# Moving the reloads of spilled FFN blocks from SyncE's queue to ScalarE's

## The chip, the cores and the metric

The kernel runs on one NeuronCore of a Trainium2 chip. Its time is device microseconds (us) from launch to end of one execution. A profile of one execution gives what each engine and each DMA queue did.

## The reference

The input x is 4 batches of 1024 tokens with 512 features. Each token gets a conditioned linear layer, then a two-layer network with simulated 8-bit quantization, then a residual sum:

```
relation = relu([x, mean(x), cond] @ W + b)               # 512 features
xq = round(relation / s_in) clipped to 0..255             # s_in = max(relation)/255
h  = relu(xq @ round(w1/s_w1).T  (scaled) + b1)           # 2048 features
hq = round(h / s_h) clipped to 0..255                     # s_h = max(h)/255, over ALL tokens
y  = hq @ round(w2/s_w2).T (scaled) + b2                  # 512 features
out = x + y
```

The scale s_h needs the maximum of h over all 4096 tokens. So all of h (4096 x 2048 in float32, 32 MB) has to exist before the first element of it can be rounded. The on-chip memory holds half of that.

## The kernel before, in words

Tokens are worked on in NB = 8 blocks of TB = 512. Weights and activations are held transposed, with 128 features on the partitions. There are three stages: the conditioned layer (to about 100 us), the first FFN product with the spill (to about 207 us), and the second FFN product. The change is in the third stage.

**Spill.** Blocks are numbered anew in this last stage: blocks 0 to 3 of the third stage lie in the four slots of `hidden` (SLOTS = 4, 4 MB each). Blocks 4 to 7 had been computed first and written to `hidden_spill` in device memory, in quarters of 1 MB (`spill_quarter`, L382). They are read back by `reload(n)` (L426), four DMAs of 1 MB each, into the slots that `SLOT = (0, 1, 2, 3, 1, 2, 3, 1)` names: block 4 into slot 1, block 5 into slot 2, block 6 into slot 3, block 7 into slot 1 again. Slot 0 is used for other sums by then.

**Third stage, per engine.** All engines follow fixed instruction orders; semaphores join them.

- ScalarE (L995 to L1007) rounds block after block: 16 ACTIVATEs of 128x512 each from `hidden` into `hid_low[n % 2]`, which is two buffers that the page calls `pool_q` (even blocks) and `w_t` (odd blocks). Before block n it waits that TensorE has finished block n-2 (the buffer is free), and for n >= 4 that the reload has landed. VectorE rounds one tile of block 0 and half of block 1.
- TensorE multiplies: blocks 0, 1, 3, 5, 7 plainly (L805, 64 matmuls of 512 columns; L815 is in `folded`), blocks 2, 4, 6 in a scheme with seven products in place of eight (`folded`, L808; each half has seven products named 1a, 5a, 6a, 3a, 7a, 2a, 4a, then the same with b). Product 5a reads sums of quarters of the hidden block that VectorE makes; product 6a adds into the bank that VectorE has just copied from (`k1a`).
- VectorE makes these sums (`sum_hidden(n, h)`, L1322, once per half of the hidden tiles), copies and combines the banks of the folded block (`finish_folded`, L1338, lines L1345, L1353, L1356), and adds bias, scale and x for the plain blocks (`finish`, L1317). Order around block 2: `finish(1, 0)`, `sum_hidden(2, 0)`, `sum_hidden(2, 1)`, `finish(1, 1)`, then `finish_folded(2)`, which begins with the copy k1a (L1345).
- GpSimd adds x to the results of blocks 0, 2, 4, 6 (L559).
- SyncE issues every DMA of this stage, in one order (L447 to L462): reload(4); store(0), wait for it to land, load x for block 4; reload(5); store(1), wait for it to land, load x for block 5; reload(6); store(2), wait, load x for block 6; reload(7); store(3), wait, load x for block 7; store 4 to 6; the last block's five pieces.

A store into `out` is issued after the block's last row is summed; the x of block n+4 goes into the place that store(n) has emptied, hence the wait.

Of the kernel before, what the change touches and what calls it, by code (L numbers as in the profile page):

```python
# [17 lines left out]
TB = 512  # L18
# [11 lines left out]
def adaln_quantized_ffn(nc, x, cond, cond_w, cond_b, w1, b1, w2, b2, out):  # L30
# [24 lines left out]
    SLOTS = NB // 2  # L55
    FQ = FT // 4
    WC = 4 * D
    HALF = TB // 2
    HB = FT * TB
# [16 lines left out]
    spill = nc.dram_tensor("hidden_spill", [SLOTS, P, HB], F32, kind="Internal").ap()  # L76

    with ExitStack() as ctx:
        def sb(name, shape, dt=F32, stack=ctx):
            return stack.enter_context(nc.sbuf_tensor(name, shape, dt))  # L80

        def sem(name):
            return ctx.enter_context(nc.semaphore(name))
# [49 lines left out]
        hidden = sb("hidden", [P, SLOTS * HB])  # L133
# [20 lines left out]
        FG, HK = FT // 2, KD // 2  # L154
# [99 lines left out]
        h_done = sem("h_done")  # L254
        h_taken = sem("h_taken")
        spilled = [sem("spilled0"), sem("spilled1")]
        reloaded = [sem("reloaded0"), sem("reloaded1")]
        xres_landed = [sem("xres_landed0"), sem("xres_landed1")]
        s_quant_ready = sem("s_quant_ready")
        first_hid_ready = sem("first_hid_ready")  # L260
        hid_ready = sem("hid_ready")
# [17 lines left out]
        SLOT = (0, 1, 2, 3, 1, 2, 3, 1)  # L279
# [26 lines left out]
        def products_to(n, name=None):  # L306

            return len(PRODUCTS) * FOLDED.index(n) + (PRODUCTS.index(name) + 1 if name else 0)
# [10 lines left out]
        def tiles_to(n):  # L319
            return sum(len(tiles) for tiles in ACT_TILES[:n])  # L320
# [5 lines left out]
        def _(sp):  # L326
# [96 lines left out]
            for par in range(2):  # L423
                sp.wait_ge(spilled[par], 16 + 16 * FQ * SLOTS // 2)

            def reload(n):  # L426

                if n == SLOTS:
                    sp.wait_ge(first_hid_ready, 2 + FG)
                    sp.wait_ge(hid_ready, tiles_to(2))  # L430
                else:
                    sp.wait_ge(hid_ready, tiles_to({5: 3, 6: 4, 7: 5}[n]))
                for q in range(FQ):
                    sp.dma_start(hidden[:, SLOT[n] * HB + q * 4 * TB:SLOT[n] * HB + (q + 1) * 4 * TB],  # L434
                                 spill[n - SLOTS, :, q * 4 * TB:(q + 1) * 4 * TB]).then_inc(reloaded[n % 2], 16)

            def store(n):
                slot = n % SLOTS
                if n in BY_POOL:
                    sp.wait_ge(summed, TJ * (BY_POOL.index(n) + 1))  # L440
                else:
                    sp.wait_ge(y_taken, TJ * (n // 2 + 1))
                sp.dma_start(out_blocks[(n + SLOTS) % NB],
                             x_res[:, slot * WC:(slot + 1) * WC].rearrange("p (j d) -> p j d", d=D)
                             ).then_inc(stored[n % 2], 16)

            reload(SLOTS)  # L447
            for n in range(SLOTS):
                if n > 0:
                    reload(SLOTS + n)  # L450
                store(n)
                sp.wait_ge(stored[n % 2], 16 * (n // 2 + 1))
                sp.wait_ge(xres_landed[n % 2], 16 * (SLOTS // 2 + n // 2))
                sp.dma_start(x_res[:, n * WC:(n + 1) * WC].rearrange("p (j d) -> p j d", d=D), x_blocks[n]
                             ).then_inc(xres_landed[n % 2], 16)
            for n in range(SLOTS, NB - 1):
                store(n)
            for i, (j, _, cols) in enumerate(last_pieces):
                sp.wait_ge(y_taken, TJ * (NB // 2 - 1) + i + 1)
                sp.dma_start(out_blocks[SLOTS - 1, :, j, cols],  # L460
                             x_res[:, (SLOTS - 1) * WC + j * D + cols.start:(SLOTS - 1) * WC + j * D + cols.stop]
                             ).then_inc(stored[1], 16)  # L462
# [100 lines left out]
        def _(pe):  # L563
# [148 lines left out]
            def part1(G):  # L712
                x11, _, x21, _ = x_quarters(PAIRS[G // FG][0])
                if G % FG == 0:
                    pe.wait_ge(act_q_ready, 2 * (G // FG) + 3)
                if G < 3:
                    pe.wait_ge(h_taken, old_tile(3 * G))
                else:
                    pe.wait_ge(c21_taken, G - 2)
                part(1, G, W11, x11, R1[G % 3], start=True)  # L720

            def part2(G):
                _, _, x21, _ = x_quarters(PAIRS[G // FG][0])
                if G < 2:
                    pe.wait_ge(h_taken, old_tile(3 * G + 1))
                else:
                    pe.wait_ge(c11_taken, G - 1)
                part(2, G, W12, x21, R2[G % 2], start=True)
# [167 lines left out]
        def _(act):  # L896
# [95 lines left out]
            act.wait_ge(s_h_ready, 1)  # L992
            act.activation(s_quant[:, :], s1[:, :], ACT.Copy, scale=s_h_inv[:, 0:1]).then_inc(s_quant_ready, 1)
            act.wait_ge(s_quant_ready, 1)
            for n in range(NB):  # L995
                if n < 2:
                    act.wait_ge(hid_filled, 4 * (n + 1))
                elif n - 2 in FOLDED:
                    act.wait_ge(fold_done, products_to(n - 2, PRODUCTS[-1]))
                else:  # L1000
                    act.wait_ge(y_done, TJ * (PLAIN.index(n - 2) + 1))
                if n >= SLOTS:
                    act.wait_ge(reloaded[n % 2], 16 * FQ * ((n - SLOTS) // 2 + 1))
                for ft in ACT_TILES[n]:
                    act.activation(hid_low[n % 2][:, ft, :],  # L1005
                                   hidden[:, SLOT[n] * HB + ft * TB:SLOT[n] * HB + (ft + 1) * TB],
                                   ACT.Copy, scale=s_quant[:, ft:ft + 1]).then_inc(hid_ready, 1)  # L1007


        @block.vector  # L1010
# [427 lines left out]
```

## Time and profile before

| | |
|---|---|
| median of 3 runs | 325.99 us (324.81 to 328.0) |
| the profiled execution, its own time | 325.08 us |
| its span, first to last instruction | 323.3 us |
| TensorE busy | 311.8 us, 96% of the span |
| VectorE busy | 272.8 us, 84% |
| ScalarE busy | 200.6 us, 62% |
| GpSimd busy | 114.9 us, 36% |
| granted TensorE clock | 1.0 of full speed throughout |
| DMA: hidden_spill, written and read back | 16 + 16 DMAs of 1 MB, median 9.8 us from issue to landing |

The profiled execution's own time is 1.8 us longer than its span: that much lies outside the first and last instruction. Times below are counted from the start of the span. PE is TensorE, DVE VectorE, ACT ScalarE, POOL GpSimd, SP SyncE; a name with a q (SPq, ACTq) is the engine's instruction sequencer, which issues the DMAs.

### The profile page before, as it was taken

How to read it: one execution, taken by the hardware profiler on the slowest of the kernel's cores; microseconds unless marked ns; L12 is line 12 of the kernel's file. 1: busy time of each engine (PE TensorE's matmuls, PEld its weight loads, DVE VectorE, ACT ScalarE, POOL GpSimd, SP SyncE). 2: the span in 40 equal slices, each digit the busy share in tenths (PEclk: the TensorE clock that was granted, in tenths of full speed). 3: DMA queues.
4: the chain of work that ended last, by engine and by line, in shares of the span. 5: the costliest groups of instructions: out<-in, count | busy, mean ns of one | idle time of the engine just before them, and what ended most of it. 6: DMA issues, size and time to landing. Idle time of an engine off the chain costs nothing.

```text
span 323.3 us, 4733 instructions
## 1 busy us (share of the span) xinstructions
PE 311.8 (96%) x1635; PEld 194.4 (60%) x1635; DVE 272.8 (84%) x602; ACT 200.6 (62%) x356; POOL 114.9 (36%) x96
## 2 busy tenths in 40 slices
PE   6999999999999999999999999899999999998695
PEld 6888888888686444444444444344478468457444
DVE  1698989997886699999999999899999699598555
ACT  2435785588377994556666662199867957744800
POOL 1076525634350699990360002602404103302400
PEclk9999999999999999999999999999999999999999
DMA  6999999999963397997980250332969979497772
GB/s 228 204 246 244 234 194 242 256 233 344 299 139 67 67 280 48 402 404 296 418 335 0 85 177 0 132 130 81 403 200 411 338 297 382 180 420 284 272 281 97
DMA packets 51624, 75.57 MB, mean 234 GB/s; under 512 B 20344, under 2 KB 34960, under 8 KB 46864
## 3 DMA queue, kind: packets, MB, share of 16 engines
q1 hardware_dynamic: 51408, 74.99, 77.3%
q10 hardware_dynamic: 192, 0.28, 0.3%
q8 instruction: 13, 0.21, 0.3%
q14 instruction: 11, 0.09, 0.1%
HBM read 45.89 MB, written 25.17 MB: 220 GB/s over the span
## 4 chain that ended last, share of the span: by engine, by line
PE 68%; DMA 14%; ACT 7%; DVE 7%; issue 2%; SPq 1%; ACTq 0%; DVEq 0%
PE bank L578 27%; PE bank L703 20%; DMA hidden<-hidden_spill 9%; PE bank L805 9%; PE bank L675 6%; ACT pool_q L1005 4%; DMA out_dram<-pool_r 4%; ACT w_t L1005 3%; DVE hidden L1179 2%; PE bank L690 2%; DMA x_in<-in_x_dram 1%; PE bank L573 1%; SPq L434 1%; PE bank L569 1%; DVE bank L1309 1%
## 5 line engine op out<-in xcount | busy, mean ns | idle before, releaser
L805 PE MATMUL bank<-w_t 128*128 128x512 f16 (+1 forms) x272 | 56.0, 367 | 2.9 <-ACT w_t L1005 2.9
L1179 DVE TENSOR_SCALAR_CACHE_REDUCE hidden<-bank,qb,hmax 128x512 f32<-128x512 f32 x62 | 47.6, 807 | 6.4 <-PE bank L703 3.8
L483 POOL TENSOR_TENSOR x_lo<-hidden,x_hi 128x512 fp32r<-128x512 f32 x28 | 35.3, 1292 | 45.8 <-ACT x_hi L899 45.8
L578 PE MATMUL bank<-x_lo,cw_hi 128*128 128x512 f32 x128 | 48.4, 389 | 0.0
L578 PE MATMUL bank<-x_hi,cw_lo 128*128 128x512 f32 x128 | 48.4, 389 | 0.0
L578 PE MATMUL bank<-x_hi,cw_hi 128*128 128x512 f32 x128 | 48.3, 392 | 0.0
L559 POOL TENSOR_TENSOR pool_r<-pool_r,steps 128x512 f32<-128x512 f32 x16 | 20.2, 1273 | 76.1 <-DVE steps L1356 60.5
L1199 DVE CUSTOM_DVE_ANT_0 hidden<-hidden,bank,hmax 128x512 f32<-128x512 f32 x66 | 45.9, 743 | 0.2
L805 PEld LDWEIGHTS bank<-w_t 128*128 128x128 f16 x272 | 26.5, 98 | 31.4 <-ACT w_t L1005 3.2
L1005 ACT ACTIVATE w_t<-hidden,s_quant 128x512 uint8<-128x512 f32 x56 | 34.8, 710 | 16.7 <-DMA hidden<-hidden_spill 8.9
L1005 ACT ACTIVATE pool_q<-hidden,s_quant 128x512 uint8<-128x512 f32 x63 | 39.0, 710 | 6.4 <-DMA hidden<-hidden_spill 3.8
L703 PE MATMUL bank<-pool_r,pool_q 128*128 128x512 f16 x144 | 36.3, 379 | 0.0
L907 ACT ACTIVATE pool_r<-pool_q,winv 128x512 int8<-128x512 f32 x28 | 17.9, 711 | 21.4 <-DVE winv L1063 21.4
L703 PE MATMUL bank<-pool_r,w_t 128*128 128x512 f16 x116 | 30.3, 379 | 0.0
L1040 DVE STREAM_TRANSPOSE hidden<-x_in 128x512 f32<-128x512 f32 x28 | 28.4, 1074 | 0.7 <-DMA x_in<-in_x_dram 0.7
L578 PEld LDWEIGHTS bank<-x_hi,cw_hi 128*128 128x128 f32 x128 | 24.0, 188 | 5.8 <-DVE hidden L1045 0.8
L578 PEld LDWEIGHTS bank<-x_hi,cw_lo 128*128 128x128 f32 x128 | 24.0, 188 | 5.1
L578 PEld LDWEIGHTS bank<-x_lo,cw_hi 128*128 128x128 f32 x128 | 24.0, 188 | 4.9
L1045 DVE TENSOR_SCALAR_CACHE_REDUCE hidden<-bank 128x512 f32<-128x512 f32 x31 | 20.2, 675 | 5.6 <-PE bank L578 5.5
L703 PEld LDWEIGHTS bank<-pool_r,pool_q 128*128 128x128 f16 x144 | 14.1, 98 | 17.0
L899 ACT ACTIVATE x_hi<-hidden 128x512 fp32r<-128x512 f32 x28 | 17.5, 624 | 9.5 <-DVE hidden L1040 9.3
L972 ACT ACTIVATE hidden<-bank,qb 128x512 f32<-128x512 f32 x22 | 15.1, 687 | 12.9 <-PE bank L703 12.9
(157 smaller groups left out, 508.7 us busy)
## 6 DMA issues: line engine op xcount, KB each, us to landing
hidden_spill<-hidden SPq DMA_DIRECT2D x16, 1024.0 KB, 9.8
hidden<-hidden_spill SPq DMA_DIRECT2D x16, 1024.0 KB, 9.8
x_in<-in_x_dram SPq DMA_DIRECT2D x32, 256.0 KB, 7.0
pool_r<-in_x_dram SPq DMA_DIRECT2D x8, 1024.0 KB, 5.3
pool_q<-in_L_ffn_w_dram SPq DMA_DIRECT2D x7, 1024.0 KB, 10.2
out_dram<-pool_r SPq DMA_DIRECT2D x7, 1024.0 KB, 10.5
pool_r<-in_L_cond_W_dram SPq DMA_DIRECT2D x2, 1024.0 KB, 10.1
x_in<-in_L_ffn_w_dram SPq DMA_DIRECT2D x1, 1024.0 KB, 5.8
```

Of the source, the lines that this page charges most:

```text
L483: pool.tensor_tensor(x_lo[:, n % 2, k, :], x_t[:, k, :], x_hi[:, n % 2, k, :].bitcast(F32), ALU.subtract).then_inc(lo_ready, 1)
L559: pool.tensor_tensor(xs, xs, out_rows[:, j, :], ALU.add).then_inc(summed, 1)
L578: return pe.matmul(REL[ot][:, :], w[:, k, ot * P:(ot + 1) * P], v[:, n % 2, k, :], start=(k == 0 and w is cw_hi and v is x_hi), stop=(k == ...
L675: mm = pe.matmul(bank[ft % BANKS][:, :], w1_t[:, ft, k, :], act_q[:, bass.ds(n * (KD * TB) + k * TB, TB)], start=(k == 0), stop=(k == KD - 1))
L703: mm = pe.matmul(to[:, :], w[:, G % FG, k, :], v[:, k * TB:(k + 1) * TB], start=(start and k == 0), stop=(k == HK - 1), skip_group_check=n ...
L805: return pe.matmul(y_bank[:, cols], hid_q[n % 2][:, ft, j * P:(j + 1) * P], w2_t[:, ft, cols], start=(ft == 0), stop=(ft == FT - 1))
L907: act.activation(w_steps[:, j * D:(j + 1) * D], w_rows[c][:, j * D:(j + 1) * D], ACT.Copy, scale=winv[:, c % 2 + c // (NB - 1), t:t + 1]). ...
L1005: act.activation(hid_low[n % 2][:, ft, :], hidden[:, SLOT[n] * HB + ft * TB:SLOT[n] * HB + (ft + 1) * TB], ACT.Copy, scale=s_quant[:, ft:f ...
L1040: dve.transpose(x_t[:, k, :].rearrange("p (q i) -> p q i", i=R), squares[:, k, :, :]).then_inc(x_turned, 1)
L1045: dve.tensor_scalar(raw[:, (n * KD + ot) * TB:(n * KD + ot + 1) * TB], REL[ot][:, :], 1.0, None, ALU.mult, ALU.max, accum_out=raw_max[:, n ...
L1179: dve.tensor_scalar(hidden[:, at:at + TB], y_bank[:, :], qb1[:, ft:ft + 1], hmax[:, ft:ft + 1], ALU.add, ALU.max, accum_out=hmax[:, ft:ft ...
L1199: dve.tensor_tensor_reduce(tile, tile, y_bank[:, :], 1.0, hmax[:, ft:ft + 1], ALU.add, ALU.max, accum_out=hmax[:, ft:ft + 1]).then_inc(tak ...
```

## The change

The reloads leave SyncE's list. ScalarE issues them, each after it has rounded the block that held the slot: reload(4) after block 1, reload(5) after block 2, reload(6) after block 3, reload(7) after block 4. Before each, ScalarE waits that its own roundings up to that block are complete. The four reloads get a semaphore each, in place of two shared by turns. SyncE's list of stores and loads of x keeps its order, with the reloads gone from it.

```diff
-        reloaded = [sem("reloaded0"), sem("reloaded1")]
+        reloaded = [sem(f"reloaded{n}") for n in range(SLOTS)]
...
@@ SyncE @@
-            def reload(n):
-
-                if n == SLOTS:
-                    sp.wait_ge(first_hid_ready, 2 + FG)
-                    sp.wait_ge(hid_ready, tiles_to(2))
-                else:
-                    sp.wait_ge(hid_ready, tiles_to({5: 3, 6: 4, 7: 5}[n]))
-                for q in range(FQ):
-                    sp.dma_start(hidden[:, SLOT[n] * HB + q * 4 * TB:SLOT[n] * HB + (q + 1) * 4 * TB],
-                                 spill[n - SLOTS, :, q * 4 * TB:(q + 1) * 4 * TB]).then_inc(reloaded[n % 2], 16)
-
...
-            reload(SLOTS)
             for n in range(SLOTS):
-                if n > 0:
-                    reload(SLOTS + n)
                 store(n)
...
@@ ScalarE @@
+            def reload(n):
+
+                if n == SLOTS:
+                    act.wait_ge(first_hid_ready, 2 + FG)
+                act.wait_ge(hid_ready, tiles_to(n - SLOTS + 2))
+                for q in range(FQ):
+                    act.dma_start(hidden[:, SLOT[n] * HB + q * 4 * TB:SLOT[n] * HB + (q + 1) * 4 * TB],
+                                  spill[n - SLOTS, :, q * 4 * TB:(q + 1) * 4 * TB]).then_inc(reloaded[n - SLOTS], 16)
+
             for n in range(NB):
...
                 if n >= SLOTS:
-                    act.wait_ge(reloaded[n % 2], 16 * FQ * ((n - SLOTS) // 2 + 1))
+                    act.wait_ge(reloaded[n - SLOTS], 16 * FQ)
                 for ft in ACT_TILES[n]:
                     act.activation(hid_low[n % 2][:, ft, :],
                                    hidden[:, SLOT[n] * HB + ft * TB:SLOT[n] * HB + (ft + 1) * TB],
                                    ACT.Copy, scale=s_quant[:, ft:ft + 1]).then_inc(hid_ready, 1)
+                if 0 < n <= SLOTS:
+                    reload(n - 1 + SLOTS)
```

## Rows read from the trace of the kernel before

**Rows 1.** The page: the span and part 1, busy us by engine.
```profile
span 323.3 us, 4733 instructions
PE 311.8 (96%) x1635; PEld 194.4 (60%) x1635; DVE 272.8 (84%) x602; ACT 200.6 (62%) x356; POOL 114.9 (36%) x96
```

**Rows 2.** TensorE's timeline, third stage: start us, length us, what [idle before <-releaser].
```profile
237.75 1.91 PE L815 MATMUL bank<-hidden 128*128 128x256 f16 x16
...
249.11 13.98 PE L805 MATMUL bank<-w_t 128*128 128x512 f16 x64
262.92 1.04 PE L815 MATMUL bank<-w_t,pool_q 128*128 128x256 f16 x8
...
275.45 13.98 PE L805 MATMUL bank<-w_t 128*128 128x512 f16 x64
289.26 1.04 PE L815 MATMUL bank<-w_t,pool_q 128*128 128x256 f16 x8
...
292.08 1.05 PE L815 MATMUL bank<-hidden 128*128 128x256 f16 x8 [0.91 <-DVE steps L1345]
...
305.64 14.03 PE L805 MATMUL bank<-w_t 128*128 128x512 f16 x80 [2.90 <-ACT w_t L1005]
```

**Rows 3.** ScalarE's timeline: rounding of blocks 2, 3, 4, 6 and 7.
```profile
223.27 9.91 ACT L1005 ACTIVATE pool_q<-hidden,s_quant 128x512 uint8<-128x512 f32 x16 [0.21 <-PE bank L805]
237.08 9.92 ACT L1005 ACTIVATE w_t<-hidden,s_quant 128x512 uint8<-128x512 f32 x16 [3.90 <-PE bank L805]
249.31 9.91 ACT L1005 ACTIVATE pool_q<-hidden,s_quant 128x512 uint8<-128x512 f32 x16 [2.31 <-PE bank L815]
...
276.87 9.91 ACT L1005 ACTIVATE pool_q<-hidden,s_quant 128x512 uint8<-128x512 f32 x16 [3.83 <-DMA hidden<-hidden_spill]
295.67 9.91 ACT L1005 ACTIVATE w_t<-hidden,s_quant 128x512 uint8<-128x512 f32 x16 [8.89 <-DMA hidden<-hidden_spill]
```

**Rows 4.** SyncE's queue, timeline: the four groups of reload issues.
```profile
223.15 2.04 SPq L434 DMA_DIRECT2D hidden<-hidden_spill  x4
...
240.48 2.34 SPq L434 DMA_DIRECT2D hidden<-hidden_spill  x4
...
259.52 2.34 SPq L434 DMA_DIRECT2D hidden<-hidden_spill  x4
...
279.75 2.21 SPq L434 DMA_DIRECT2D hidden<-hidden_spill  x4
```

**Rows 5.** The chain of waits that ended last, two steps: start us, length us, what.
```profile
233.22 0.70 DVE hidden L1331
...
246.91 12.16 DMA out_dram<-pool_r
```

**Rows 6.** VectorE's timeline: k1a of block 2, and first sum of block 4's second half.
```profile
238.03 0.42 DVE L1345 TENSOR_TENSOR steps<-bank,ends_b 128x256 f32<-128x256 f32 x1
...
259.70 0.69 DVE L1331 TENSOR_TENSOR hidden<-pool_q 128x1024 f16<-128x1024 f16 x1
```

**Rows 7.** DMA issues on ScalarE's queue at the start, and the ScalarE instruction behind them.
```profile
0.73 0.41 ACTq L927 DMA_DIRECT2D pool_r<-in_L_cond_W_dram  x1
...
2.48 1.28 ACT L934 ACT_TABLE_LOAD   x1 [2.48 <-issue]
```

**Rows 8.** Issue durations (ns) of reloads and spills, and the reloads' us from issue to landing.
```profile
L434 SPq DMA_DIRECT2D hidden<-hidden_spill x16: 339/441/832, 223.1 to 281.5; - x16
DMA to landing us min/median/max: 4.9/9.8/15.4
...
L383 SPq DMA_DIRECT2D hidden_spill<-hidden x16: 319/332/1454, 112.6 to 159.8; - x16
```

**Rows 9.** Busy by stretch: length, PE, PEld, DVE, ACT, POOL busy; clock, DMA share, GB/s.
```profile
223.20:236.90 13.70, 13.70 (x66) 6.19 (x64) 13.16 (x21) 9.91 (x16) 5.08 (x4) 1.00 0.93 342
...
262.90:275.40 12.50, 12.37 (x113) 10.83 (x112) 11.13 (x26) 9.91 (x16) 2.56 (x2) 1.00 1.00 392
275.40:289.20 13.80, 13.80 (x66) 6.29 (x65) 10.18 (x17) 9.91 (x16) 2.49 (x2) 1.00 0.71 279
```

## The prediction

> **What bounds the kernel now.** The page comes first: TensorE is busy 96% of the span [rows 1]. So only two things can shorten the time: less work for TensorE, which the change doesn't touch, or fewer stalls of it. TensorE's own timeline of the third stage shows where they are. From 223 us on it runs without a gap until block 6, where it loses 0.91 us on a VectorE copy, and 2.90 us ahead of block 7, on ScalarE's rounding [rows 2]. That is 3.81 us in all.
>
> ScalarE's timeline says why. Block 6 was rounded from 276.87 and block 7 from 295.67, and both had waited for a reload to land (3.83 and 8.89 us); blocks 2, 3 and 4 had waited for TensorE alone [rows 3]. SyncE's queue says why the reloads were late: the slot of block 6 was free when block 3 was rounded, at 237.08 + 9.92 = 247.00, but its reload was issued at 259.52; the slot of block 7 was free at 249.31 + 9.91 = 259.22, and its reload was issued at 279.75 [rows 3, 4]. In between SyncE stood waiting for a store to land, one of which took 12.16 us on the chain of waits [rows 5].
>
> **What the change gives.** With the reloads on ScalarE's queue their issue no longer stands behind a store. What it is worth is read from block 4, the last folded block whose data was there in time: TensorE took 275.45 - 262.92 = 12.53 us for it. Block 6 began at 289.26 and block 7 at 305.64, which is 16.38 us [rows 2]. With block 6 at the pace of block 4 the gain is 16.38 - 12.53 = **3.85 us**. Two conditions: rounding of block 6 starts when TensorE frees the buffer (with block 5's first product at 275.45, as block 4's did with block 3's), and rounding of block 7 starts when block 5 is done (289.3) and ends 9.9 us later at 299.2, ahead of 289.26 + 12.53 = 301.8. Both hold if the transfers land by 275 and 289. They would be issued near 247.5 and 261 (below) and the longest reload so far took 15.4 us from issue to landing [rows 8], so they land by 265 and 279 with ten us to spare. What would be late next behind block 7's rounding is nothing for 2.6 us.
>
> **What the change costs on ScalarE.** Four issues lie between two roundings. ScalarE's queue keeps order: at the start of the kernel its first engine instruction begins at 2.48, once its DMA issues are through, and one such issue is 0.41 us [rows 7]. SyncE needs 2.04 to 2.34 us for four reload issues [rows 4], 0.34 to 0.83 us each [rows 8]. The bounds for a group on ScalarE are zero (were the issue to run beside the engine, against which rows 7 speak) and four times the longest issue of that size on any queue, a spill's 1.454 us, so 5.8 us [rows 8]. I take 2.04 us, the same four DMAs at the same moment on SyncE's queue. A group by itself cannot be below zero in cost.
>
> Now each of the four places:
>
> - reload(4), behind block 1. SyncE issued it at 223.15 [rows 4], so its transfer moves by nothing. But ScalarE began block 2 at 223.27 with only 0.21 us idle before it [rows 3]: there is no hole for the issues. Rounding of block 2 begins at 223.15 + 2.04 + 0.04, about 225.2, **1.95 us later**, and ends at 235.1. VectorE started the sums of block 2's second half at 233.22, as ScalarE ended at 233.18 [rows 3, 5]; from there it works in its fixed order up to k1a, which ended at 238.03 + 0.42 = 238.45 [rows 6]. TensorE's 16 matmuls from 237.75, in 1.91 us, are products 5a and 6a, so 6a, which waits for k1a, began about half way, near 238.65 [rows 2]. The slack is 0.2 us. VectorE is busy 13.16 of 13.70 us there [rows 9] and makes up nothing. So 6a, and with it all of TensorE's work behind it, is late by 1.95 - 0.2 = **1.75 us**; with the uncertainty of a boundary that the row doesn't show, 1.7 to 1.95, and I take 1.8.
> - reload(5), behind block 2: issued 235.2 to 237.4. ScalarE had 3.90 us idle before block 3 [rows 3]; it now starts that block at 237.4 in place of 237.08 and ends at 247.3, while TensorE wants it only at 249.11 + 1.8 [rows 2]. Zero; cover left 3.6 us.
> - reload(6), behind block 3: 247.4 to 249.6. Block 4's rounding waits for TensorE to end block 2, which was 249.1 and will be 250.9 [rows 2]. Zero; cover left 1.3 us.
> - reload(7), behind block 4 (now ends 261.0): 261.1 to 263.3, while block 5's rounding waits for TensorE until 262.92 + 1.8 [rows 2]. Zero; cover 1.4 us.
>
> ScalarE's new wait for its own roundings is in these times (SyncE's go for reload(4) included the same wait). Queued behind it is only the next rounding. The four semaphores cost nothing; nobody reads them but ScalarE.
>
> **What it moves on SyncE.** 16 issues go, 8.9 us of its queue in four groups [rows 4], none of which ran while anyone waited for SyncE except a reload. Stores and loads of x come earlier or stay. They now share the DMA engines with reloads issued beside them. From 235 to 291 us there are 12 MB of reloads, 3 stores and 3 loads of x, 1 MB each, so about 18.9 million bytes; at the 392 GB/s that the busiest stretch shows [rows 9] this is 48 of 56 us. It fits, and it is not tight before 277, by when two of the three reloads are due.
>
> Here a rule of the Trainium skill speaks against the change. DMA: Bandwidth & Descriptors, "Issuing engines are not separate DMA queues", says that DMAs started by different engines run on the same 16 DMA engines and interleave, so that a second issuer saves only sequencer time. By it alone the sum would have no gain of 3.85 us. The trace has the reason to set it aside here: the DMA engines stood idle for part of the time while the reloads waited, with a share of 0.71 over block 5 against 1.00 before it [rows 9]. What is gained is the earlier issue, not bandwidth.
>
> **The sum.** -3.85 + 1.8 = -2.05 us. Against the profiled execution 325.08 - 2.05 = 323.0. That execution lies 0.9 us below the median of the runs, 325.99; against the median it is 323.9. I give **323.8**, 0.7% below the median.
>
> **Rivals.**
>
> 1. *The issues are hidden.* If ScalarE's issues cost its rounding nothing, or VectorE takes up the delay, the whole 3.85 us stays: 325.99 - 3.85 = 322.1, 1.2% less. For it: at a gap between two roundings nothing shows a DMA issue delaying an ACTIVATE. Against it: rows 7, and VectorE's full load [rows 9]. Chance 0.13.
> 2. *ScalarE's issue group becomes the bound (slower).* Its place is the second group: block 2's rounding, reload(5), block 3's rounding and reload(6) then form one chain without a hole. With d the delay of block 2, block 4's rounding starts at 233.19 + d + 0.1 + (d + 0.08) + 9.92 + 0.1 + (d + 0.08) = 243.5 + 3d in place of 249.31, with 259.70 - 259.22 = 0.5 us of slack at VectorE [rows 3, 6]. TensorE's loss is the larger of d - 0.2 and 3d - 6.3. It eats the 3.85 us at d = 3.4, that is at a group of 3.5 us or 0.87 us an issue: just above the longest reload issue (0.832), under the longest spill issue (1.454) [rows 8]. At 1.0 us an issue the loss is 5.5, the sum +1.6: 327.6. At 1.454, d = 5.7, the loss is 10.9 and the time 333. Against it: the first reload group on an idle queue took 0.51 an issue. Chance 0.12, half of it beyond 1% slower.
> 3. *The transfers don't come sooner.* The reloads share the 16 DMA engines with stores, and the two last land when they did before; the early cost remains: 325.99 + 1.8 = 327.8. This needs 29 us from issue to landing for block 6 and 34 for block 7, where 15.4 is the longest [rows 8]. The Trainium skill's rule named above would have it so. Chance 0.05.
> 4. *Only one stall goes*, by a wait I don't see (x arriving late for block 5 or 6, since each store now shares its engines with a reload): block 6's 0.9 us or block 7's 2.9 us stays, and the sum is between -1.1 and +0.9: 325 to 327. Chance 0.1.
>
> My forecast has 0.6.
>
> **How the numbers follow.** A difference under 1% (3.3 us) cannot be told from none by a measurement like this. The forecast, the fourth and most of the third are within it; the first is just outside, and runs of one kernel spread over 3 us. Faster by over 1%: 0.13 times three quarters, plus a little of the forecast's 0.6: 0.17. Slower by over 1%: half of the second and a little of the third, 0.08. Within: 0.75. The range takes in the hidden issues against the profiled execution (325.08 - 3.85 = 321.2) at the low end, and the lesser stall and the mild form of the second rival at the high end: 321.3 to 327.0.
>
> **What would show it.** Reload issues on ScalarE's queue near 223.1, 235.2, 247.4 and 261, each group near 2 us. Block 2's rounding from 225.2. A new TensorE stall of 1.7 to 1.95 us at product 6a of block 2, near 238.6, released by VectorE's L1345. Block 5's products from 277.3 in place of 275.45. No stall at block 6 or ahead of block 7, which starts at 303.6 in place of 305.64. ScalarE's waits before blocks 6 and 7 ended by TensorE, not by a DMA. Wrong would be: no stall in block 2 (the first rival), stalls at block 4 released by ScalarE (the second), a DMA that still releases block 6 or 7 (the third).

## The result, and the profile after

The changed kernel takes 323.44 us in the median of 13 runs (322.83 to 324.38), the kernel before 326.48 us in 13 runs (324.81 to 329.15). The ratio is 0.9908, 95% interval 0.9884 to 0.9933: a gain of 3.0 us. The profiled execution took 323.03 us, 2.05 us less than the one before; its span is 321.2 us. Two runs of the kernel before in the experiments below, 331.75 and 332.15 us, lay over 1.5% above its fastest and are left out of the ratios and of the comparison by clock.

ScalarE's timeline of the third stage, changed kernel (start us, length us, what [idle before <-releaser]); ACTq rows are the reload issues on its queue:

```profile
223.06 1.99 ACTq L988 DMA_DIRECT2D hidden<-hidden_spill  x4
225.10 9.92 ACT L1001 ACTIVATE pool_q<-hidden,s_quant 128x512 uint8<-128x512 f32 x16 [2.12 <-issue]
235.05 1.90 ACTq L988 DMA_DIRECT2D hidden<-hidden_spill  x4
237.01 9.91 ACT L1001 ACTIVATE w_t<-hidden,s_quant 128x512 uint8<-128x512 f32 x16 [1.99 <-PE bank L791]
246.95 1.78 ACTq L988 DMA_DIRECT2D hidden<-hidden_spill  x4
251.12 9.92 ACT L1001 ACTIVATE pool_q<-hidden,s_quant 128x512 uint8<-128x512 f32 x16 [4.20 <-PE bank L801]
261.07 1.77 ACTq L988 DMA_DIRECT2D hidden<-hidden_spill  x4
...
277.47 9.91 ACT L1001 ACTIVATE pool_q<-hidden,s_quant 128x512 uint8<-128x512 f32 x16 [2.62 <-PE bank L801]
291.28 9.91 ACT L1001 ACTIVATE w_t<-hidden,s_quant 128x512 uint8<-128x512 f32 x16 [3.90 <-PE bank L791]
```

Beside [rows 3] one sees both halves. Blocks 6 and 7 are now released by TensorE, not by a DMA. Block 2 starts 1.83 us later than before, and what ended its idle time is "issue": its own queue's four DMAs.

TensorE's timeline, changed kernel, around the folded blocks:

```profile
237.68 1.04 PE L801 MATMUL bank<-hidden 128*128 128x256 f16 x8
240.32 1.05 PE L801 MATMUL bank<-hidden 128*128 128x256 f16 x8 [1.60 <-DVE steps L1343]
...
250.92 13.98 PE L791 MATMUL bank<-w_t 128*128 128x512 f16 x64
264.73 1.04 PE L801 MATMUL bank<-w_t,pool_q 128*128 128x256 f16 x8
...
277.26 13.98 PE L791 MATMUL bank<-w_t 128*128 128x512 f16 x64
291.08 1.04 PE L801 MATMUL bank<-w_t,pool_q 128*128 128x256 f16 x8
...
303.61 14.02 PE L791 MATMUL bank<-w_t 128*128 128x512 f16 x80
```

Product 6a of block 2, a stretch without a gap before [rows 2], waits 1.60 us for VectorE's copy k1a. The idle entry is less than what was lost: from the start of block 2 (236.81 here, 236.88 before) to that of block 3 TensorE took 14.11 us against 12.23, which is 1.88 us more, and block 5 starts 1.81 us later than before (277.26 against 275.45). The stalls of 0.91 and 2.90 us at blocks 6 and 7 are gone: block 7 starts at 303.61 in place of 305.64.

SyncE's queue, changed kernel: stores (L432) and loads of x (L440).

```profile
229.71 0.38 SPq L432 DMA_DIRECT2D out_dram<-pool_r  x1
239.79 0.37 SPq L440 DMA_DIRECT2D pool_r<-in_x_dram  x1
248.73 0.38 SPq L432 DMA_DIRECT2D out_dram<-pool_r  x1
266.74 0.37 SPq L440 DMA_DIRECT2D pool_r<-in_x_dram  x1
```

A load of x follows as soon as the store before it has landed, so store(1) took 266.74 - 248.73 = 18.0 us, where it took 12.16 before [rows 5]. That was not forecast; it comes back below. The load of x for block 4, issued at 239.79, landed only 17.2 us later, at 257.0, so store(1) stood behind it on SyncE's own queue.

### The profile page after: what moved, and what is told of

It reads as the page before. It is cut to its first block, busy times and chain, and to the rows that moved or that the text cites. A ratio compares the mean times of both kernels' runs of the same rounds, so it can differ in the third digit from the quotient of the medians.

```text
span 321.2 us, 4733 instructions
## 1 busy us (share of the span) xinstructions
PE 311.8 (97%) x1635; PEld 194.3 (61%) x1635; DVE 272.5 (85%) x602; ACT 200.6 (62%) x356; POOL 114.9 (36%) x96
## 4 chain that ended last, share of the span: by engine, by line
PE 76%; DVE 11%; ACT 8%; issue 2%; DMA 1%; ACTq 1%; DVEq 0%
PE bank L564 27%; PE bank L689 21%; PE bank L801 10%; PE bank L791 6%; PE bank L661 6%; ACT pool_q L1001 6%; DVE hidden L1177 2%; PE bank L676 2%; DVE bank L1307 2%; ACT w_t L1001 2%; DMA x_in<-in_x_dram 1%; DVE bank L1302 1%; PE bank L559 1%; DVE hidden L1331 1%; DVE hidden L1329 1%
## 5 line engine op out<-in xcount | busy, mean ns | idle before, releaser
L545 POOL TENSOR_TENSOR pool_r<-pool_r,steps 128x512 f32<-128x512 f32 x16 | 20.3, 1275 | 77.2 <-DVE steps L1354 61.6
L689 PEld LDWEIGHTS bank<-pool_r,pool_q 128*128 128x128 f16 x144 | 14.1, 98 | 17.0
L958 ACT ACTIVATE hidden<-bank,qb 128x512 f32<-128x512 f32 x22 | 15.1, 687 | 12.9 <-PE bank L689 12.9
```

The costliest lines, as they stand in the source:

```text
L545: pool.tensor_tensor(xs, xs, out_rows[:, j, :], ALU.add).then_inc(summed, 1)
L689: mm = pe.matmul(to[:, :], w[:, G % FG, k, :], v[:, k * TB:(k + 1) * TB], start=(start and k == 0), stop=(k == HK - 1), skip_group_check=n ...
```

## The experiments

Theory: the four issues behind block 1 cost 1.6 us on the path through block 2, the other three groups nothing, and the earlier issue of reload 6 and 7 takes away both old stalls. Rivals are those of the prediction. Each run has its own set of runs of the kernel before, on the same chip.

### The parts of the change, one by one

**reload(4) stays on SyncE**, the others go to ScalarE:

```diff
@@ SyncE, ahead of store(0), with the waits that reload(4) had @@
+            for q in range(FQ):
+                sp.dma_start(... spill[0, quarter q] ...).then_inc(reloaded[0], 16)
@@ ScalarE @@
-                if 0 < n <= SLOTS:
+                if 1 < n <= SLOTS:
                     reload(n - 1 + SLOTS)
```

> The changed kernel, but reload(4) is issued by SyncE as before; reload(5) to (7) stay on ScalarE. Theory: the four issues behind block 1's rounding cost TensorE 1.7 us at product 6a of block 2, the other three groups cost nothing. So block 2's rounding starts near 223.2, the stall of 1.60 us at 6a is gone, and the time is 1.7 us under the changed kernel's, the full 3.85 us or more under the kernel before. Rival (the other groups cost too, or the stall is VectorE's own): the stall stays and the time is that of the changed kernel within 0.5 us.

321.35 us (321.0 to 322.33) against 326.64: ratio 0.983 (0.979 to 0.987). The list of all of TensorE's waits from 209 us on has one entry left, which every kernel here has at the stage's start:

```profile
PE bank L796 <- DVE pool_q L1272: 0.4, 1, 0.4
```

As the theory had it. It was run again beside the changed kernel itself.

> The changed kernel, unchanged, beside the next ones on the same chip. A second profile of it: the stall of 1.60 us at product 6a of block 2 and no other; its runs spread over under 2 us, those of the kernel before over more, since only the latter's end hangs on the landing of stores.

> The kernel with reload(4) on SyncE and (5) to (7) on ScalarE, on the same chip as the changed kernel. Theory: 1.6 us under the changed kernel, the length of its one stall. Rival (part of the 2.1 us between their medians so far came from different chips or sets of runs): the difference is under 1.0 or over 2.2 us.

On that chip the changed kernel took 323.67 us (322.72 to 324.19) and this one 321.84 (320.9 to 322.04): 1.8 us for the one group of issues. The kernel before spread from 325.75 to 330.29 there (and once 331.75), four and a half us against one and a half. The second profile of the changed kernel has the same single new stall, 1.5 us.

**Only reload(4) goes to ScalarE**; reload(5) to (7) stay in SyncE's list:

```diff
@@ SyncE @@
-            reload(SLOTS)
@@ ScalarE, in the loop over blocks @@
+                if n == 1:
+                    ... the same waits and four act.dma_start of reload(4)
```

> The kernel before, but reload(4) alone is issued by ScalarE (behind block 1's rounding); reload(5) to (7) stay in SyncE's list behind the stores; a semaphore for each reload. Theory: only the cost is left: a stall of 1.6 to 1.9 us at product 6a of block 2, store(1) and all behind it later by as much, the stalls at blocks 6 and 7 as before: 1.8 us slower than the kernel before (between 1.6 and 2.0). Rival (stalls at blocks 6 and 7 absorb it, since the reload lands at its own time): no difference to the kernel before.

325.46 us against 326.64, ratio 0.996 (0.993 to 0.999). The expectation of 1.8 us more was wrong, and its rival right. TensorE's waits:

```profile
PE bank L804 <- ACT w_t L1004: 1.9, 1, 1.9
PE bank L814 <- DVE steps L1350: 1.6, 1, 1.6
```

The stall of 1.6 us in block 2 is there, but behind it TensorE's old stalls have shrunk from 3.81 to 1.9 us. In this order the end hangs on reload(7), whose rounding starts at 296.06 here and at 295.67 before [rows 3], and that does not move when TensorE is late. So the cost of the issues is real only once the old stalls are gone: cost and gain are not two independent terms. Their sum in the prediction holds because the gain was read to a TensorE without stalls behind block 2. That the median is even 0.4% lower goes with the granted clock, which every run lists. Eleven of the twelve runs of this kernel had a mean clock of 0.999 or 1.00, with a median of 325.44 us; of the kernel before on that chip 6 of 23 had 1.00, with a median of 325.34, and the rest 0.983 to 0.995. At full clock the two are the same. The section on the missing microsecond takes this up.

**Only the semaphores**, one for each reload:

> The kernel before with a semaphore for each reload in place of two shared ones, nothing else. Theory: no difference (within 0.3 us); a second profile of that order of work. Where its time lies above the first profile's 325.08, the excess is in the stalls ahead of blocks 6 and 7 (3.81 us in all there), since only these hang on the landing of stores. Rival (the shared semaphores let a rounding start early or late): a difference of over 1 us; or the excess is spread over stretches before 223 us.

326.96 against 326.64 us, ratio 1.000 (0.996 to 1.003). They cost nothing and bring nothing. All other kernels of this study that differ in the reloads have them too.

**All reloads on SyncE, in the order in which their slots come free:**

```diff
@@ SyncE @@
+            reload(4)
+            store(0)
+            reload(5)
+            next_x(0)        # wait for store 0 to land, load x for block 4
+            store(1)
+            reload(6)
+            next_x(1)
+            reload(7)
+            store(2)
+            next_x(2)
+            store(3)
+            next_x(3)
```

> All reloads issued by SyncE, in the order in which their slots come free: reload 4, store 0, reload 5, load x 0, store 1, reload 6, load x 1, reload 7, store 2, load x 2, store 3, load x 3; ScalarE issues none. Theory: the gain comes from the order alone, not from who issues: no stall at 6a of block 2, none at blocks 6 and 7, 3.85 us or more under the kernel before, equal to the kernel with reload 4 on SyncE and the rest on ScalarE within 0.5 us. Rival (a queue of its own is what counts: on one queue the reload stands behind store 1 and load x 1 and lands late): a stall of over 1 us stays before block 6 or 7, and the gain is under 3 us.

321.37 us (321.03 to 322.32), ratio 0.983 (0.979 to 0.987), no stall from 209 us on but the common 0.4. So the gain is that of the order. A second queue is not needed for it, and without it ScalarE has nothing to pay. This is faster than both kernels.

### The price of an issue

**Eight DMAs of 512 KB, and one of 4 MB, in place of four of 1 MB**, both on ScalarE's queue:

```diff
-                for q in range(FQ):
-                    act.dma_start(hidden[:, ... 4 * TB floats ...], spill[...])
@@ the first kernel: 8 DMAs @@
+                for q in range(2 * FQ):
+                    act.dma_start(hidden[:, ... 2 * TB floats ...], spill[...])
@@ the second kernel: 1 DMA @@
+                act.dma_start(hidden[:, SLOT[n] * HB:(SLOT[n] + 1) * HB], spill[n - SLOTS, :, :])
```

> The changed kernel with each reload split into eight DMAs of 512 KB in place of four of 1 MB; same bytes, same places. It doubles the suspected cost. Theory (an issue costs ScalarE about 0.45 us whatever its size): a group takes 3.6 us, block 2's rounding starts 3.6 us late, and now the chain block 2 rounding, reload(5), block 3 rounding, reload(6) has no hole: by the formula of the second rival, 3d - 6.3, TensorE loses 4.5 us by block 4 in place of 1.6: 2.9 us slower than the changed kernel, near 326.3, with a stall at block 4 as well. Rival (the time goes by bytes, 4 MB a group): a group stays at 2 us and the time does not change.

> The changed kernel with each reload as one DMA of 4 MB. Theory (cost by the DMA): a group takes 0.5 us, block 2's rounding starts 0.5 us late, the stall at product 6a is 0.3 us at most, and the time is 1.3 to 1.6 us under the changed kernel's, near 322.0. Rival (by bytes): 2 us for the issue, the same stall of 1.6 us, no change.

The first group of issues and block 2's rounding, with eight DMAs, then with one:

```profile
223.04 3.91 ACTq L988 DMA_DIRECT2D hidden<-hidden_spill  x8
227.00 9.92 ACT L1001 ACTIVATE pool_q<-hidden,s_quant 128x512 uint8<-128x512 f32 x16 [4.05 <-PE bank L791]
```

```profile
223.84 0.36 ACTq L987 DMA_DIRECT2D hidden<-hidden_spill  x1
224.25 9.91 ACT L1000 ACTIVATE pool_q<-hidden,s_quant 128x512 uint8<-128x512 f32 x16 [0.49 <-PE bank L791]
```

3.91 us for eight, 1.99 for four, 0.36 for one, all for 4 MB: ScalarE pays by the DMA, 0.36 to 0.50 us each here, not by the byte. Both rivals about bytes fall.

With eight the time was 328.56 us against 327.23, ratio 1.004 (1.000 to 1.008); the expected 326.3 was missed by 2.3 us in the median, and the profiled execution, 326.8, is the fastest of its ten. That is where the second rival of the prediction put its turning point: the whole gain eaten at groups of 3.5 us and more. By block 7's start, 307.37, it is 3.76 us behind the changed kernel's profile where 2.9 was expected, and the parts are others than forecast. TensorE's stall at 6a is 3.25 us, and then the clock is found at its lower level. TensorE's windows (length, busy by engine, clock, DMA share, GB/s):

```profile
240.00:242.00 2.00, 0.00 (x0) 0.00 (x0) 1.86 (x4) 0.67 (x2) 0.00 (x0) 1.00 1.00 379
242.00:244.00 2.00, 1.77 (x9) 1.28 (x10) 1.71 (x4) 2.00 (x5) 0.00 (x0) 0.57 1.04 395
244.00:246.00 2.00, 2.00 (x13) 1.47 (x12) 1.17 (x3) 2.00 (x4) 0.00 (x0) 0.58 0.99 352
246.00:250.00 4.00, 4.00 (x39) 3.60 (x37) 3.86 (x10) 4.00 (x8) 1.28 (x1) 1.00 1.03 402
```

Block 2 takes 254.38 - 237.06 = 17.3 us there against 250.92 - 236.81 = 14.1 in the changed kernel: 1.65 us more of stall and some 1.6 us of slow products. The second, longer chain of my formula added only 0.43 us of stall at block 4; the slow products of block 2 had delayed TensorE already, which left that chain less to add.

With one DMA each the stall at 6a is gone as forecast, but the time is 325.71 us, ratio 0.995 (0.992 to 0.998), 3.7 above the expected 322.0. What VectorE and TensorE waited for, with one DMA each:

```profile
DVE pool_r L1312 <- DMA pool_r<-in_x_dram: 3.4, 1, 3.4
```

```profile
PE bank L801 <- DVE steps L1342: 3.4, 1, 3.4
```

and the chain of waits that led there:

```profile
230.48 20.73 DMA out_dram<-pool_r
...
251.64 26.91 DMA out_dram<-pool_r
...
278.56 6.30 DMA pool_r<-in_x_dram
...
284.89 0.03 DVE pool_r L1312
```

Two stores took 20.73 and 26.91 us to land, the x of block 5 came 3.4 us late, and VectorE's fixed order handed that to TensorE in block 6. This is the prediction's fourth rival, in a neighbour of the kernel: an x that comes late and makes a stall in block 6.

**The same single DMAs, on SyncE in the order of need:**

> All reloads on SyncE in the order of need, each as one DMA of 4 MB. With one DMA each on ScalarE's queue a store took 27 us to land, the x of block 5 came late, and TensorE stalled 3.4 us. Theory: the store suffered because a long-row reload on another queue takes most of what the DMA engines give; on the same queue it waits its turn and no more, so every store lands within 21 us, no stall, 321.4 us. Rival (it is the 4 MB DMA itself that holds up what comes behind or beside it): a late x and a stall of over 1 us here too.

321.05 us (321.03 to 321.49), ratio 0.981 (0.974 to 0.987), no stall, stores landing within 20.7 us; store(1) in 8.4. So the large DMA does no harm on the store's own queue. These two kernels differ in more than the queue: on ScalarE's queue reload(6) was issued 3.9 us ahead of store(1), here 0.4 us behind it. A cleaner pair is the kernel with reload(4) on SyncE and the others on ScalarE, and the one with all on SyncE in order, both with four DMAs a reload. In both store(1) and reload(6) are issued within half a microsecond of each other, at 247; the row below each store is the load of x that waits for its landing. Reloads on ScalarE's queue, then on SyncE's:

```profile
247.07 0.38 SPq L432 DMA_DIRECT2D out_dram<-pool_r  x1
270.63 0.37 SPq L445 DMA_DIRECT2D pool_r<-in_x_dram  x1
```

```profile
246.90 0.39 SPq L443 DMA_DIRECT2D out_dram<-pool_r  x1
...
256.19 0.38 SPq L450 DMA_DIRECT2D pool_r<-in_x_dram  x1
```

The store took 23.6 us with the reload on the other queue and 9.3 us with it on its own. A store that is issued behind a reload on its own queue waits as well: store(2), behind reload(7), took 20.3 us with four DMAs and 20.7 with one, there without a stall. The median of 321.05 us is the lowest of the study, though the runs of the kernels with 321.35 and 321.37 us overlap with it and were made on another chip.

### Which queue, and in which order

**reload(7) alone on ScalarE**, behind block 4; the others in the old list:

```diff
@@ SyncE @@
-                if n > 0:
+                if 0 < n < SLOTS - 1:
                     reload(SLOTS + n)
@@ ScalarE, in the loop over blocks @@
+                if n == SLOTS:
+                    ... wait for its roundings, four act.dma_start of reload(7)
```

> The kernel before with reload(7) alone on ScalarE, behind block 4's rounding; reload(4) to (6) stay in SyncE's list behind the stores; a semaphore for each reload. Theory: ScalarE has over 3 us to spare there, so it costs nothing and takes away the stall ahead of block 7 (2.9 to 3.3 us); the one at block 6 (0.9 to 1.8 us) stays. 2.9 us or a little more under the kernel before, some 1.0 to 1.8 over the 321.4 of the kernels without any stall. Rival (reload 7, issued beside reload 6 on another queue, takes its bandwidth, and block 6 comes later by several us): a stall at block 6 of over 3 us and a gain of under 1.5 us.

332.67 us (332.11 to 333.44), ratio 1.016 (1.013 to 1.019): 5.4 us slower. The theory was wrong, the rival right. ScalarE's rounding of blocks 6 and 7:

```profile
286.12 9.91 ACT L1005 ACTIVATE pool_q<-hidden,s_quant 128x512 uint8<-128x512 f32 x16 [12.78 <-DMA hidden<-hidden_spill]
295.93 9.89 ACT L1005 ACTIVATE w_t<-hidden,s_quant 128x512 uint8<-128x512 f32 x16
```

TensorE's waits and one of its stretches behind them:

```profile
PE bank L815 <- ACT pool_q L1005: 6.4, 1, 6.4
PE bank L815 <- DVE steps L1350: 1.6, 1, 1.6
```

```profile
296.00:301.00 5.00, 3.57 (x16) 2.26 (x16) 4.78 (x9) 5.00 (x10) 0.00 (x0) 0.50 0.58 153
```

SyncE issued reload(6) at 259.79, as late as ever, and ScalarE reload(7) at 259.55. They shared the DMA engines: the longest DMA of the two reloads took 24.6 us from issue to landing, where it had been 15.4 [rows 8]. Block 6's data, needed first, came at 286 in place of 276.9, and block 7's lay ready long before its turn. TensorE stood for 8.0 us in two stalls and ran at half clock between them and for a while after.

**reload(6) and (7) on ScalarE**, (4) and (5) on SyncE in the old list:

> The kernel before with reload(6) and (7) on ScalarE, behind the roundings of blocks 3 and 4; reload(4) and (5) stay on SyncE in the old list. It tells why reload(7) alone on ScalarE cost 5 us. Theory: there reload(7) shared the DMA engines with a reload(6) that had been issued no sooner on the other queue, though block 7 is needed 14 us after block 6; on one queue they go in order. So now neither block waits: no stall at blocks 6 and 7, 321.4 us, equal to the kernel above. Rival (reload(7) so early harms whatever queue reload(6) is on): a stall of over 1 us at block 6 or 7.

323.65 us (322.12 to 325.61), ratio 0.988 (0.982 to 0.995). Neither reload is waited for any more, though reload(7) was issued as early as before (259.80), so an early reload(7) does no harm by itself: what cost the 5 us was that it shared the engines with a reload(6) issued no sooner. The step to the other queue and the earlier issue of reload(6), 247.57 in place of 259.79, came together here; no run parts them. But a stall of 1.6 us came up that I hadn't expected:

```profile
DVE pool_r L1321 <- DMA pool_r<-in_x_dram: 1.6, 1, 1.6
```

store(1), issued at 247.46 behind reload(5) on its own queue and beside reload(6) on the other, landed after 25.8 us, and the x of block 5 was late again.

### The missing microsecond

The medians differ by 3.0 us, the two profiles by 2.05.

> The kernel before, unchanged, for a further profile. Theory of the extra microsecond (the measured gain is 3.0 where the profile pair shows 2.05): the kernel before's stalls at blocks 6 and 7 vary from execution to execution with the landing of stores, and the first profile, with 3.81 us, was one of the short ones. So profiled time minus 325.08 should go with the sum of the two stalls minus 3.81, apart from what happens before 223 us. Rival: the stalls are 3.8 us whatever the time, and the excess lies elsewhere.

There are now three profiles of the old order and two of the changed one. The stalls are those of TensorE at blocks 2, 6 and 7; the start is where the first reload is issued.

| profile | time | start of the first reload | time less start | stalls |
|---|---|---|---|---|
| before | 325.08 | 223.15 | 101.9 | 3.81 |
| before again | 324.64 | 223.25 | 101.4 | 3.3 |
| semaphores alone | 327.09 | 223.86 | 103.2 | 5.1 |
| changed | 323.03 | 223.06 | 100.0 | 1.6 |
| changed again | 323.84 | 224.04 | 99.8 | 1.5 |

In the old order the time behind the start goes with the stalls: 1.8 us apart in both, to within 0.1. The two profiles of the changed kernel differ by 0.2 us there. So the old order's end varies with the landing of its transfers. The profile from which I predicted lay 0.9 to 2.2 us under the medians of the old kernel (325.99 to 327.23).

The stalls are not the whole of it. The mean granted clock parts the two orders as well. It is listed for the runs of the kernel before on the three chips of the experiments and for all runs of the changed kernel:

| kernel, mean granted clock | runs | median | range |
|---|---|---|---|
| before, 1.00 | 9 | 325.57 | 324.74 to 326.81 |
| before, 0.983 to 0.995 | 42 | 327.20 | 325.75 to 330.29 |
| changed, 0.998 or 1.00 | 19 | 323.51 | 322.72 to 324.38 |

At full clock the difference is 2.06 us, as forecast. The old order has the full clock in about one run of six, the changed one has it or 0.998 in every run, and the rest of the gain goes with that. The size fits: a mean of 0.995 over 325 us, if it comes from a stretch at half speed, is 3.3 us of such a stretch and so 1.6 us lost (an estimate from the listed clock); the 22 runs with 0.995 have a median of 326.75, 1.2 us over those with 1.00. All three profiles of the old order are of executions at 1.00, so where in the kernel the clock fell was not seen. Behind the longer stalls of two other kernels here it was found at its lower level (last section), and a longer stall at block 6 or 7 with slow products behind it would do the same; that is likely, not shown.

## Why the prediction was right

Point by point, with its own steps:

- **The issue group on ScalarE**, taken at 2.04 us: 1.99 in the first group, 1.77 to 1.90 in the others. That it holds up the rounding (the first rival denied it) is shown by the "issue" entry ahead of block 2, and by the run with one DMA, where the issue takes 0.36 us and the idle time before block 2 grew only from 0.21 to 0.49 us.
- **The cost at product 6a**, 1.75 us with a range of 1.7 to 1.95, taken as 1.8: right. The idle entry there is 1.60 us in one profile and 1.5 in the other, but block 5 started 1.81 us later, and two medians of one chip differ by 1.8. The idle entry counts from the end of product 5a, 1.04 us after its start, where without a stall the next product starts after 0.87 us; and the two products behind the stall start 0.93 us apart.
- **The other three groups cost nothing**: right, TensorE ends ScalarE's wait behind each (1.99, 4.20 and 3.90 us idle in all). Behind reload(5) it was close: 1.90 of the 1.99 us are the issues, so ScalarE itself had no time left; the prediction's cover of 3.6 us lay behind it, in how early TensorE needs block 3.
- **The gain of 3.85 us**: block 6 took 303.61 - 291.08 = 12.53 us, exactly block 4's pace, in place of 16.38.
- **The places**: block 5's products at 277.26 (277.3 forecast), block 7's at 303.61 (303.6).
- **The sum**: -2.05 us between the profiles, as forecast. The medians differ by 3.0. The mis-sized term is the gain of 3.85 us: the old kernel's stalls, 3.81 us in the profile I had, are 5.1 in another, and five in six of its runs have a lower granted clock, which the prediction didn't count at all. The gain was read to 0.01 us from one execution of a kernel whose end hangs on DMAs; that its runs already spread over 3.2 us should have told me that the gain does too, and that it would rather be larger than smaller, since the profile lay under their median. That the forecast of 323.8 is within 0.4 us of 323.44 has luck in it: I took a gain of 2.2 us off a median of three runs, 325.99, and the median of 13 was 326.48. The two errors, 0.8 us of gain and 0.5 us of start, go against each other.
- **The rivals**: the first is refuted. The second is no part of the changed kernel, and its turning point (a group of 3.5 us) is borne out by the run with eight DMAs at 3.9, though some 1.6 us of its price was the clock, which I hadn't counted. The third is refuted: both reloads landed in time. Its price was wrong too: if the last two reloads had landed when they did before, the 1.8 us would have gone into the old stalls, as in the run with reload(4) alone on ScalarE, and the time would have stayed near 326, not risen to 327.8.
- **Wrong without effect**: "stores and loads of x come earlier or stay". store(1) landed 5.9 us later after its issue than before, and the x of block 5 was requested 7.7 us later (266.74 against 259.09 on SyncE's queue). I had counted bytes against bandwidth, found it "not tight before 277", and not asked how two queues share; in the changed kernel the DMA share was 1.01 to 1.03 from 246.9 to 273, which is full. The changed kernel got through it without a stall: the x of block 5 landed 11.6 us after its issue, at 278.3, and VectorE came to it at 282.5. Two of its neighbours didn't, by 3.4 and 1.6 us. I had given this course 0.1, as the fourth rival.
- **The threshold**: "a difference under 1% cannot be told from none" was too careful. With 13 runs each the interval is 0.9884 to 0.9933, and the 0.9% stand clear of none.

## What to carry to other kernels

When a transfer comes late, look first at what its issue stands behind: here a wait for a store in a fixed list cost 12 and 20 us of issue time, and reordering the list was worth more than moving it to another engine. A DMA issue on a compute engine is free only where that engine has a hole; price it by the number of DMAs, not the bytes, and check what hangs on the instruction behind it. Transfers that are needed in an order belong on one queue in that order. When large transfers move to a second queue, all that the first has still to move becomes slower together, so a transfer there that somebody waits for should have nothing ahead of it. And a profile from which a stall is read should be one whose time and granted clock are those of most runs.

## What the runs showed of the hardware

**Two queues do not share evenly.** While ScalarE's queue has reloads to move, SyncE's queue gets about a quarter of the DMA engines' time, and what it has been given waits in line for that. store(1) is 1 MB in rows of 2 KB. Ahead of it on SyncE's queue stands the load of x for block 4, issued 0.4 to 13 us earlier. The last column is what SyncE's queue moved in a stretch inside the store's wait, in millions of bytes, with its part of the 16 engines' time:

| reload(6): queue, rows | x of block 4 landed | store(1) issued | took | SyncE's queue meanwhile |
|---|---|---|---|---|
| SyncE, 8 KB | 252.9 | 246.90 | 9.3 us | alone |
| SyncE, 32 KB | 252.0 | 246.77 | 8.4 us | alone |
| ScalarE, 4 KB | 253.4 | 252.19 | 12.9 us | 1.05 in 11.5 us, 23.5% |
| ScalarE, 8 KB (changed) | 257.0 | 248.73 | 18.0 us | 1.54 in 16.5 us, 24.2% |
| ScalarE, 8 KB (changed again) | 257.8 | 249.58 | 19.8 us | 1.57 in 18.5 us, 22.0% |
| ScalarE, 8 KB (reload(4) on SyncE) | 259.0 | 247.07 | 23.6 us | 2.03 in 22.0 us, 24.1% |
| the same again | 260.0 | 247.65 | 23.8 us | 2.03 in 22.0 us, 24.1% |
| ScalarE, 32 KB | 268.5 | 251.64 | 26.9 us | 2.10 in 26.0 us, 22.9% |

So the store's time goes with the bytes that its own queue has still to move, at 81 to 93 GB/s, and not plainly with the rows on the other queue: beside rows of 8 KB it is 18.0 to 23.8 us. An influence of the rows is not excluded. From 252 to 260, beside rows of 32 KB, SyncE's queue moved 0.10 million bytes in 8 us (5.5%); from 250 to 258, beside rows of 8 KB with reload(4) on SyncE, 1.08 million (35.3%). With a reload unfinished ahead of it on its own queue store(1) took 10.7 to 12.7 us when ScalarE's queue was empty (the old order), and 25.8 when it was not (reload(6) and (7) on ScalarE). The Trainium skill, DMA: Bandwidth & Descriptors, "Queues, rings and completion order", says that each DMA engine takes turns between its queues packet by packet. The traces agree that both queues are served at once; why one gets three quarters, no run here shows.

**TensorE's clock after a stall.** Behind the stall of 3.25 us the granted clock was 0.57 over 4 us, and the eight matmuls of a product took 1.88 us in place of 1.05. In the run with reload(7) alone it was 0.50 from 296 to 301, behind the stall of 6.44 us, and 0.61 from 301 to 306, behind that of 1.59. Those are the lower of its levels, 1.2 of 2.4 GHz, for most of the stretch. Behind the stall of 2.90 us before the change [rows 2], and 3.42 us with one DMA each, the products ran at the full pace, so the length of the stall alone does not tell which it will be. Where the clock falls, a stall of this size can cost half as much again: 1.6 us on top of 3.25.
